# Three moves inside one iteration: the Bm part on TensorE, gate's and the sixth tanh on ScalarE, the turned context on VectorE

## The reference, cut to what matters

```
xn  = layernorm(x)
per token t:  r = decay * r + c_t * c_t ;  retained = xn_t * r      (c: the context)
              inp  = retained @ Wi.T + bi
              gate = sigmoid(inp @ Wg.T + bg)
              state = tanh((gate * state + (1 - gate) * inp) @ A.T + inp @ Bm.T)
              out  = state @ Wo.T + bo
x1  = x + tanh(g_xattn) * out
ffn(z) = swiglu(z @ sh) @ so + sum over the 2 best of 8 experts e: p_e * (swiglu(z @ w1) @ w2[e])
y   = x1 + tanh(g_ffn) * ffn(layernorm(x1))
```

## Time and profile before

| | |
|---|---|
| Median of 3 runs | 482.99 us (482.75 to 483.21) |
| The profiled execution | 483.19 us, of which 481.4 us span |
| Mean granted TensorE clock | 0.985 |
| Busy: PE, DVE, ACT, POOL | 431.2, 367.7, 221.1, 180.4 us |

### The profile page before, as it was taken

The page is one execution under the profiler, slowest core; times in us unless marked ns, Lnnn a source line. Parts: engine busy times, 40 slices in busy tenths (PEclk is TensorE's granted clock), DMA queues, the critical chain, the costliest instruction groups (busy, mean ns, idle before and its releaser), DMA issues.

```text
span 481.4 us, 12175 instructions
## 1 busy us (share of the span) xinstructions
PE 431.2 (90%) x4344; PEld 353.6 (73%) x4344; DVE 367.7 (76%) x1318; ACT 221.1 (46%) x518; POOL 180.4 (37%) x217
## 2 busy tenths in 40 slices
PE   5987699899988989999989889998999999989881
PEld 4974588777877878988778779887777676765540
DVE  2587979898989776777879768778867758556796
ACT  3564556676745454646355446453524133322100
POOL 3011302342437521102366664412635235526720
PEclk9999889999999999999999999999999999999996
DMA  6795050514234363653341199872311067696431
GB/s 159 197 246 155 2 152 3 142 31 127 52 127 115 127 127 87 137 123 80 99 123 45 45 183 217 181 148 89 124 42 46 34 127 163 142 227 193 146 113 65
DMA packets 99531, 57.05 MB, mean 118 GB/s; under 512 B 72080, under 2 KB 90000, under 8 KB 99472
## 3 DMA queue, kind: packets, MB, share of 16 engines
q1 hardware_dynamic: 95120, 44.72, 38.7%
q0 software_dynamic: 4352, 11.54, 8.1%
HBM read 23.22 MB, written 24.51 MB: 99 GB/s over the span
## 4 chain that ended last, share of the span: by engine, by line
PE 50%; DVE 29%; issue 7%; ACT 3%; POOL 3%; DMA 2%; DVEq 0%; POOLq 0%; ACTq 0%
PE bank L583 12%; PE bank L572 11%; PE bank L630 6%; PE rec L714 5%; PE rec L597 4%; DVE u_hi L1306 4%; PE bank L858 3%; DVE u_full L1308 3%; PE rec L630 2%; DVE r L1416 2%; PE rec L602 2%; PE rec L572 2%; DVE raw_w L1324 2%; ACT state L995 2%; DVE ret L1429 1%
## 5 line engine op out<-in xcount | busy, mean ns | idle before, releaser
L995 ACT ACTIVATE state<-rec 128x64 f32<-128x64 f32 x128 | 36.6, 286 | 165.3 <-PE rec L602 165.2
L1306 DVE SCALAR_TENSOR_TENSOR u_hi<-gt,state 128x64 f16<-128x64 f32 x127 | 38.8, 305 | 66.2 <-ACT state L995 65.7
L1875 POOL DMA_INDIRECT hrows<-hid_rows,slots_i x44 | 51.2, 1163 | 79.9 <-ACT state L995 45.3
L597 PE MATMUL rec<-u_hi,a_hi 128*128 128x32 f16 x512 | 47.8, 194 | 15.8 <-DVE u_hi L1306 15.7
L1888 POOL DMA_INDIRECT yg<-yrows,slots_i x44 | 45.1, 1025 | 39.9 <-ACT state L995 29.3
L597 PEld LDWEIGHTS rec<-u_hi,a_hi 128*128 128x128 f16 x512 | 37.0, 98 | 24.6 <-DVE u_hi L1306 20.0
L597 PE MATMUL rec<-u_hi,a_lo 128*128 128x32 f16 x512 | 47.4, 193 | 0.0
L1818 POOL TENSOR_TENSOR hs_lo<-hs,hs_hi 128x512 f16<-128x512 f32 x15 | 17.3, 1154 | 57.3 <-ACT hs_hi L1196 57.3
L1308 DVE SCALAR_TENSOR_TENSOR u_full<-gt,state 128x64 f32<-128x64 f32 x127 | 37.7, 297 | 0.0
L597 PEld LDWEIGHTS rec<-u_hi,a_lo 128*128 128x128 f16 x512 | 35.1, 98 | 3.0 <-issue 0.6
L602 PE MATMUL rec<-u_lo,a_hi 128*128 128x32 f16 x512 | 36.2, 194 | 0.9
(11 more groups left out here) (299 smaller groups left out, 1418.3 us busy)
## 6 DMA issues: line engine op xcount, KB each, us to landing
x_sb<-in_x_dram SPq DMA_DIRECT2D x16, 256.0 KB, 3.2
c_sb<-in_ctx_dram SPq DMA_DIRECT2D x64, 64.0 KB, 3.0
xr_sb<-in_x_dram SPq DMA_DIRECT2D x16, 256.0 KB, 3.8
hrows<-zeros SPq DMA_DIRECT2D x4, 1024.0 KB, 6.0
yrows<-squares_w SPq DMA_DIRECT2D x16, 256.0 KB, 2.8
yrows<-squares_sh SPq DMA_DIRECT2D x15, 256.0 KB, 3.0
raw_w<-in_L_ffn_w_dram SPq DMA_DIRECT2D x8, 256.0 KB, 4.4
out_dram<-raw_w SPq DMA_DIRECT2D x8, 256.0 KB, 2.4
```

Source lines behind the costliest of these rows:

```text
L597: pe.matmul(o[:, oc, :], w[:, kc, oc * P:(oc + 1) * P], u_hi[t % 2][:, kc, :], start=False, stop=False, skip_group_check=True)
L995: act.activation(step_of(state[i % 2], t), step_of(rec[i % 2], t), ACT.Tanh, scale=1.0 / PSCALE).then_inc(st_ready, 1)
L1306: dve.scalar_tensor_tensor(out=u_hi[p][:, :, :], in0=gate, scalar=1.0, in1=old, op0=ALU.add, op1=ALU.mult).then_inc(uh_ready, 1)
L1875: pool.indirect_dma_start(hrows[q % 2], bass.IndirectOffsetOnAxis(ap=slots_i[q][:, at:at + 1], axis=0), hid_rows[t % 6][:, s, :, :].rearra ...
```

## The change: what it does

On PE the Bm part of tile a goes from slot 4 (ahead of the pair that dense iterations have there) to slot 5, between step 5 of the recurrence and the second transposition. On ACT the order behind step 4 was: x normalised, x1 normalised, gate's tanh, then step 5's tanh. It becomes: x normalised, gate's tanh, step 5's tanh, then x1 normalised. On DVE the turned context goes from slot 4, behind `max_index` and in front of `chosen`, to slot 6, the first thing behind `gated_state(i, 6)`. The work itself is the same.

```
--- before.py
+++ after.py
@@ -889,7 +889,6 @@
 
                 recurrence(i, 4, k)
                 gate_product(a, k)
-                addend_bm(a, k)
                 duos_at(i, 4)
                 if k.dense(d):
                     if k.has(c):
@@ -903,6 +902,7 @@
                     pair(0, d)
 
                 recurrence(i, 5, k)
+                addend_bm(a, k)
                 x1_transposed(c, k)
                 for q in range(len(CHUNKS)):
                     if d == last_of(q):
@@ -1228,10 +1228,10 @@
                 tanh_step(i, 4, k)
                 y_evacuated_at(i, 4)
                 x_normalised(f, k)
+                gate_tanh(a, k)
+
+                tanh_step(i, 5, k)
                 x1_normalised(c, k)
-                gate_tanh(a, k)
-
-                tanh_step(i, 5, k)
                 if k.has(c):
                     act.wait_ge(t2_done, k.n(c))
                     if k.has(c - 1):
@@ -1719,7 +1719,6 @@
                     for n in range(HALVES):
                         last = dve.max_index(top_at[:, n, :], top[:, n, :], lg[:, n, :])
                     last.then_inc(top_at_ready, 1)
-                context_turned(f, k)
                 if k.has(d):
                     dve.wait_ge(top_at_ready, k.n(d))
                     dve.tensor_copy(chosen[:, :, :], top_at[:, :, 0:2]).then_inc(chosen_ready, 1)
@@ -1764,6 +1763,7 @@
                 combined_at(i, 5)
 
                 gated_state(i, 6, k)
+                context_turned(f, k)
                 for q in range(len(CHUNKS)):
                     if d == last_of(q):
                         places(q)
```

More of the change, by code:

```diff
@@ L1230, in iteration @@
                 x_normalised(f, k)
-                x1_normalised(c, k)
                 gate_tanh(a, k)
                 tanh_step(i, 5, k)
+                x1_normalised(c, k)
                 if k.has(c):
```

## The result

| | before | after |
|---|---|---|
| Median of 5 runs | 483.15 us (482.75 to 483.22) | 488.86 us (486.45 to 489.85) |
| Profiled execution | 483.19 us | 489.85 us |
| Mean granted clock of it | 0.985 | 0.976 |

The ratio is 1.0108, with a 95% interval of 1.0078 to 1.0139: slower, by 5.7 us between the medians. (Ratios here are worked out from all runs, so they differ a little from the quotient of the two medians, which is 1.0118 in this case.)

The account below looks back on a forecast made before the run. Neither PE (50% of the chain) nor DVE (29%) alone was taken to set the time; PE waits for u_hi and xn. Gains of 2.2 against losses elsewhere summed to +5.35 us on the median 482.99: 488.3 us, range 484.4 to 490.6.

Parts of the forecast that it names:

- Iterations 13, 14, 15: Slots 4 and 5: PE idles before the pair (+1.5), then +0.6; in 15 xn behind step 5's tanh delays the transposition, +1.3.
- Iterations 5, 6, 9, 10: Slot 5: Bm fills PE's wait, step 5's tanh runs earlier, recurrence 6 follows the transposition at once: gain 0.55 each.
- Iterations 2 and 3: Slot 6: ACT's squares wait for the context, w2_high comes late, POOL's low half meets u_hi: +0.55 each.
- Iteration 4: Slots 6 and 7: same ACT delay, and the context precedes placing and odds on DVE, delaying u_hi: +0.8.
- Iteration 7: Slots 4 and 5, closed row: recurrence 5 waits for a blocked u_hi, and Bm covers tanh and xn only partly: +0.65.
- Iteration 11: Slots 4 and 5: the same as iteration 7, with u_full blocked by POOL: +0.5.
- Iterations 8 and 12: Slots 4 and 5: +0.2 each, DVE's counts coming sooner; in 12, slot 6, the context ahead of busy DVE adds +0.7.
- Iteration 1 and SP: u_hi comes just behind the gate product, and SP's later context load has nearly an iteration to spare: 0.
- B: Rival: POOL and DVE fall in the other order in iterations 2 to 4; 485.4 to 487.2 us, middle 486.3; chance 0.18.
- C: Rival: dense iterations 13 to 15 take up their loss, DVE's sums over experts bounding them: 484.9 us; chance 0.08.
- D: Rival: the hole in slot 5 of iterations 2 to 6, 9 and 10 is wholly filled: 481.2 us, faster; chance 0.10.
- E: Rival: more is lost, upper ends of iterations 2 to 4, 7, 8, 11, 12, +2.5 together: 490.8 us; chance 0.09.

Follow-up runs that it names:

- the fastest kernel: Kernel before with PE's and ACT's moves only in iterations 1, 5, 6, 9, 10 and the context late only in 5, 6, 8, 9, 10: 477.96 us, ratio 0.9901.

## Why the prediction was right, and where it was not

The result lies inside the range and 0.6 us from the forecast, but the sum is closer than its terms, and closer than the five executions lie together (486.45 to 489.85 us).

*Iterations 13, 14, 15: +1.5, +0.6, +1.3 forecast, +1.52, +0.54, +1.19 measured.* The pair waits 1.53 us for hid_lo at 347.26 where Bm's product stood; in 15 xn starts behind the tanh (411.53) and the transposition waits 1.38 us for it. With the old order back there, all of it goes. Shown.

*Iterations 5, 6, 9, 10: -0.55 each forecast, -0.91 to -1.26 measured.* The mechanism is the one named: the hole is filled but not closed (0.77 us left before the transposition), xn still starts at nr's end, and recurrence 6 follows at once. nr has not moved: in iteration 10 it starts 2.99 us later than before, in an iteration that begins 2.99 us later. The term was mis-sized. Up to step 6 it is 0.67 to 0.71: the recurrence starts 0.47 us behind the transposition (I had 0.54, before it was 1.11), and the tanh of step 6 starts 0.68 us behind that, where it was 0.76, since u_lo is there in time as well. Another 0.24 is the context's: I had its 0.69 us out of DVE's queue "under the transposition", while the low half of the recurrence and the A product wait for what stands behind it in that queue: without the context's move PE starts the low half 0.18 us later, just behind the end of u_lo, and the A product's first matmul takes 0.1 us longer, just behind the end of cn. Iteration 6 has some 0.3 more, which the context's move alone also gives.

*Iterations 2 and 3: +0.55 each forecast, +1.31 and +1.45 measured.* Again the right chain (squares behind the context, w2 behind them, POOL's low half against u_hi), with two links missing. From tanh to tanh in iteration 3 the parts are: step 6 to 7 +0.67 (3.96 to 4.63 us), since the copy (L1004, 0.31 us) stands behind the same wait as the squares, which I had left out; step 7 to the next step 0 +0.37 (1.97 to 2.34), the first low half against u_hi, which I took to be swallowed by that delay; and step 0 to 1 +0.40 (2.32 to 2.72), counted in the next iteration, because the second low half met the scan, took 0.8 us longer, and handed that to u_hi. *Iteration 4: +0.8, measured +1.38*: 0.41 up to its step 6 is that last part of iteration 3's, and 0.97 is its own. This is near the 0.8, but not for the reason given: I had put 0.69 of it at least to the context in front of the placing on DVE, "a row without a pause". With w2_high first the context is still there, and iteration 4 is at +0.07. So the row had slack, and what cost was ACT's wait and POOL's low half, as in 2 and 3. Shown.

*Iteration 7: +0.65, measured +1.04.* The wait for u_hi and the covered xn came as worked out (PE idle 0.16 at 199.35; the transposition right behind Bm). The 0.36 us behind it are the word's register load, most of which had been hidden: with the load a step earlier they are gone, and the iteration is at +0.47. That the cause is PE's sequencer, held at the wait for xn and so no longer ahead of its work, is my reading and not shown apart. *Iteration 11: +0.5, measured +0.54.* *Iterations 8 and 12: +0.2 and +0.9, measured +0.08 and +0.66.* In 12 most comes behind step 6 (+0.59), the context in front of the placing; the context alone gives +0.20, since before step 6 it takes 0.38 off.

*Iteration 1 and SP: 0.* The start of the span moved by +0.85 us and depends on the clock. SP's loads came late nowhere.

So two errors of opposite sign, -1.85 us in the waiting iterations and about +2.2 in 2 to 4, made a sum better than its terms. That they cancelled is luck: iterations 2, 3 and 4 lie beyond the upper ends that I had given them (1.0, 1.0 and 1.2).

The rivals: B (POOL and DVE in the other order) falls by the rows of iteration 3, POOL ahead of den by 0.06 us in slot 4 and of u_hi by 0.21 us behind step 7. C (the dense iterations take it up) falls by the runs with 13 to 15 as before. D (hole wholly filled) falls by the 0.77 us still there; it was right that the idle time was to be had, and the version with the moves only in the waiting iterations has 2.8 us of it. E (more is lost in 2 to 4) was right in its place, and was cancelled.

Three numbers in the working do not come out as they stand. In iterations 2 and 3 ACT's work ends near 113.7 against the tanh of 113.09, which is 0.6 and not 0.55. D takes the 1.9 us of iterations 2 to 4 out of the costs, although a sooner xn does nothing for ACT's wait for the context in slot 6; with them left in, D is at 483.1 and not 481.2. And the upper ends that E adds up come to +3.95 and not +2.5, so E would reach 492.3. None of the three changes the forecast by more than 0.1 us.

## What to carry to other kernels

A reorder in a loop is as many changes as the loop has kinds of iteration: sort them first by whether the engine waits at that place or is a closed row, and make the move only where it waits (here the same three edits are +1.1% everywhere and -1.0% in the right iterations). Waiting is not enough, though: in iterations 2 to 4 PE waits at that place too, 0.77 us for u_hi in iteration 3, and the moves on PE and ACT gain nothing there, because u_hi stands behind den on DVE, which they do not touch. When an instruction is delayed on an in-order engine, list everything behind it on its consumers too, down to the engine whose instructions were seen to hold up the critical one (here POOL's low halves and DVE's u_hi). And when work that covered a wait is taken away, ask what else it covered: here a register load and the run of a low half.

## What the runs showed of the hardware

**The lock between DVE and POOL passes on.** DVE's scan (two inputs in SBUF, 1.35 us) held POOL's low half to 1.98 us, and that held DVE's next u_hi to 1.15 us (iteration 3, above). So u_hi took 0.9 us longer than its 0.27, because the scan directly ahead of it on its own engine had put off POOL's low half, which then came in between. The Trainium skill (SBUF — State Buffer, section "Who interferes with whom") has the exclusion for the whole length of an instruction; the trace agrees, and shows the chain besides.

**A register load on PE can come out into the open.** The load of the expert word left PE idle for 0.36 us behind a transposition that started 0.14 us behind the end of its input xn, and left none when it was issued a step earlier. In the kernel before, where xn had ended 0.93 us ahead of the transposition, no idle time showed.

**The stretches at the lower clock are not the same in each execution.** The kernel after from 36 to 66 us (length; busy time of PE, PEld, DVE, ACT and POOL with their instructions; granted clock; DMA share; GB/s), and the same of the fastest kernel:

```profile
36.00:66.00 30.00, 24.46 (x186) 19.50 (x185) 22.01 (x72) 14.07 (x31) 7.05 (x8) 0.72 0.26 71
```

```profile
36.00:66.00 30.00, 23.33 (x209) 18.86 (x209) 24.82 (x78) 16.73 (x37) 7.05 (x8) 0.89 0.37 94
```

Between 36 and 66 us the mean grant was 0.72 in the one and 0.89 in the other (0.89 in the kernel before too): stretches at 1.2 instead of 2.4 GHz, in a part of the program where PE is busy for 24.46 and 23.33 of 30 us. In the other executions of the kernel after, the time goes with the mean clock: 486.45 and 487.19 us at 0.986, 488.86 at 0.979, 489.16 at 0.974. That does not hold of every kernel: with Bm alone moved there are 486.44 us at 0.990 and 483.28 at 0.986. What sets off the longer stretch was not tried.

A second place lies behind the last tanh. The traces of four kernels (ScalarE's order alone, the two that leave the context in slot 4 in all iterations and move the rest in all or up to 12, and the fastest) have 10 us there at a mean of 0.83 or 0.84 and take 1.7 to 1.9 us longer from the last tanh to the end than the kernel before; the others stay at 1.00 and differ from it by 0.7 less to 0.4 more. It is not the edit: the two kernels with the context late in 5, 6, 8, 9 and 10 have the same code from iteration 2 on, and one has +1.92, the other +0.10. Ahead of the fall PE stood still for 2 us (421 to 423 us of the fastest kernel's trace); where the clock held, PE was busy for 0.36 of the matching 2 us (425 to 427).

The five executions of the kernel after lie 3.4 us apart, and the 29 of the kernel before on one chip 5.4 us (480.30 to 485.67). This is why the terms were read from iterations 2 to 15 of the traces.
